# Rounding part of the eight-bit codes inside the attention's self half instead of ahead of it

## The chip, the cores and the metric

One Trainium2 chip, one core. The metric is device time in microseconds (us) of one execution, median of the runs shown. PE is TensorE, DVE is VectorE, ACT is ScalarE, POOL is GpSimd, SP issues most of the transfers.

## What is computed

The kernel is a two-layer decoder on x [16, 128, 256] and a context [16, 128, 256]. The change lies in one sublayer, the quantised attention of the second layer. Cut to what matters:

```
def _div_clamp_fp8(x, scale):
    y = jnp.clip(x / scale, -448, 448).astype(bfloat16)
    return y.astype(float8_e4m3fn)
q, k, v = (linear(_div_clamp_fp8(ln(x), s_j), w_j) for j in ("q", "k", "v"))   # self
qx      =  linear(_div_clamp_fp8(ln(x), s_qx), w_qx)                            # cross queries
kx, vx  =  split(ctx @ w_kv_x)
core = gqa(ln(q), ln(k), v);  xout = gqa(ln(qx), ln(kx), vx)
out  = _div_clamp_fp8(concat(core, xout), smooth) @ wproj
```

So the same normalised rows are divided by four different scale vectors and rounded to eight-bit floats, which gives four arrays of codes: query, key, value and cross query.

## The kernel before, in words

`quant_layer` runs two parts one after the other, with a barrier of all engines between them.

`round_codes` makes all codes. `XT` holds the normalised rows turned, as 2 blocks of 128 channels by 2048 tokens. There are 4 x 2 = 8 arrays (code kind by block, index n), each of 2048 columns in four tiles of 512. ACT scales an array into bf16 (L1531). DVE clamps it, takes its power of two by a mask, and makes the magic number of it (L1549, L1554, L1562, in halves of 1024). PE adds y + m - m in PSUM with three products per tile (L1521 to L1523), which does the rounding. ACT copies two of the four tiles to `xq` (L1541), DVE the other two (L1579).

`attention` runs 128 units: 8 head groups w, and for each the 16 batches b; units 0 to 63 are the self half, 64 to 127 the cross half. `in_steps` writes the order by hand: in step s each engine runs its list of stages, each for unit s minus its lag. PE: queries(s), keys_values(s), turn_p(s-3), turn_q(s-1), turn_k(s-1), output(s-5), values(s-3), scores(s-1). Every engine runs in its own order and waits on semaphores only. The PSUM banks of queries and keys have one buffer: PE's queries of unit n+1 wait until `apply_q` of unit n (L2003) has read the bank, and keys_values until `apply_kv` (L2010) has. The chain inside a step is: PE queries and keys, DVE statistics (L1992, L1997), POOL variance and power (L1947, L1952), DVE `apply_q` and `apply_kv`. Before `apply_q`, DVE runs magic (L2039), reciprocals, rounding (L2043) and residual (L2047) of older units. ACT turns queries and keys out of PSUM (L1866, L1874) for PE's scores (L1779). POOL then normalises the probabilities (L1956) and subtracts in rounded (L1963).

Of the kernel before, what the change touches and what calls it, by code (L numbers as in the profile page):

```python
# [18 lines left out]
P = 128  # L19
# [31 lines left out]
WHOLE = 1.5 * 2.0 ** 23  # L51

# [74 lines left out]
def build(nc, io, stop=99):  # L127
    ctx = ExitStack()
    with ctx:
# [13 lines left out]
        def sbuf(c, name, shape, dt):  # L143
            return c.enter_context(nc.sbuf_tensor(name, shape, dt))
# [22 lines left out]
        with ExitStack() as rows_ctx:  # L167
            XT = sbuf(rows_ctx, "XT", [P, CB, TOK], F32)
            args = dict(nc=nc, io=io, sem=sem, sbuf=sbuf, X=X, XT=XT, small=small, ident=ident, ps=ps,
                        col=col, cols=cols)  # L170
            with ExitStack() as routed_ctx:
# [1292 lines left out]
def quant_layer(row_stats, quant, rows_stored, w2_stored, nc, io, sem, sbuf, **args):  # L1464

    args = dict(nc=nc, io=io, sem=sem, sbuf=sbuf, **args)
    XT, cols, col = args["XT"], args["cols"], args["col"]
    ctx = ExitStack()
    with ctx:
        xq = sbuf(ctx, "xq", [P, 4, CB, TOK], F32R)  # L1470
        with ExitStack() as inner:
            round_codes(inner, xq, quant, **args)

        attention(xq, row_stats, quant, rows_stored, w2_stored, **args)


def round_codes(ctx, xq, quant, nc, io, sem, sbuf, X, XT, small, ident, ps, col, cols):

    N = 4 * CB
# [5 lines left out]
    p2 = sbuf(ctx, "p20", [P, 2, TOK], BF16)  # L1485
    m = sbuf(ctx, "m0", [P, 2, TOK], BF16)
# [8 lines left out]
    def bank(n, q):  # L1495
        return ps[(n * TILES + q) % 8][:, :]

    with nc.Block() as block:
# [10 lines left out]
        def _(pe):  # L1509
# [100 lines left out]
def attention(xq, row_stats, quant, rows_stored, w2_stored, nc, io, sem, sbuf, X, XT, small, ident, ps, col, cols):  # L1610
# [15 lines left out]
    with ctx:  # L1626
# [10 lines left out]
        spare = XT[:, :, :].rearrange("p k n -> p (k n)")  # L1637
# [17 lines left out]
        d_c = [sem(f"u_dc{k}") for k in range(4)]  # L1655
        names = ("cst", "chi", "clo", "q", "kv", "stat", "var", "rstd", "qn", "kvn", "tq", "tk", "qt", "kt", "sc", "neg",
# [23 lines left out]
        with nc.Block() as block:  # L1680
            @block.sync
            def _(sp):
# [20 lines left out]
                def load_context(u):  # L1703
# [132 lines left out]
            def _(act):  # L1836
                def context_high(u):
# [69 lines left out]
                in_steps([(turned_q, 2), (turned_k, 2), (prepare, 0), (context_high, 0), (scaled, 4), (row_normed, 8), (exps, 2),  # L1907
# [4 lines left out]
            def _(pool):  # L1912
# [3 lines left out]
                pool.wait_ge(s_cst, 3)  # L1916

# [61 lines left out]
                in_steps([(rounded, 5), (row_deviation, 7), (deviation, 0), (prepare, 0), (context_low, 0), (normalise, 2)])  # L1979

            @block.vector
            def _(dve):
                dve.wait_ge(s_cst, 3)

# [68 lines left out]
                def row_moments(u):  # L2053
                    if u.last:
# [4 lines left out]
                          (magic, 4), (reciprocals, 2), (rounding, 4), (residual, 5), (apply_q, 0)])  # L2059
# [655 lines left out]
```

## Time and profile before

| | us |
|---|---|
| median of 3 runs | 1412.66 |
| lowest, highest | 1412.54, 1413.17 |
| span of the profiled execution | 1411.1 |
| `round_codes`, first to last instruction | 341.94 to 370.84 |
| first PE instruction of attention | 371.58 |
| one step in the middle of the self half, PE's queries to PE's queries (568.44 to 574.10) | 5.66 |

The profiled execution has no time of its own in the records beside its span; the median of the runs is 1.6 us above that span, which is what lies around the first and the last instruction. In timelines a row is: start in us, duration in us, engine, line, operation, output<-inputs, shape, count; in brackets the idle time before it and what ended it.

### The profile page before, as it was taken

The page shows a single profiled execution, that of the slowest core. Times are in us where ns is not written, and L with a number is a line of the kernel's source. Part 1 is how long each engine was busy: PE and PEld are TensorE (multiplying, and loading weights), DVE is VectorE, ACT ScalarE, POOL GpSimd, SP SyncE. Part 2 cuts the span into 40 slices and gives each one's busy share as a digit, 9 for nine tenths or more (in the row PEclk, how much of TensorE's full clock was granted, in tenths as well). Part 3 has the DMA queues.
Part 4 walks back from the last instruction along what each step waited for, and adds up shares of the span by engine and source line. Part 5 has one row for each costly group of instructions (what it writes and reads, how often), then busy time and mean ns, then how long its engine had stood idle before and what let it go on. Part 6 is the DMA issues. An engine that isn't in the chain of part 4 may idle for free. (4 is left out here: it accounts for less than half of the span.)

```text
span 1411.1 us, 28423 instructions
## 1 busy us (share of the span) xinstructions
PE 1322.5 (94%) x8507; PEld 1098.8 (78%) x8507; DVE 1073.4 (76%) x2567; ACT 944.4 (67%) x3181; POOL 909.4 (64%) x1101
## 2 busy tenths in 40 slices
PE   9999988896799999999999999999999978999992
PEld 4445666663499999999999989998998855889882
DVE  5899768897788888888998888888888847444443
ACT  3997457776488787888887777777777746332331
POOL 4996237774178687786887767766867844455542
PEclk9999999998999999999999999999999999999996
DMA  9421110000101002002011020020100149577665
GB/s 341 158 117 63 36 46 2 1 2 1 60 1 62 29 2 98 1 31 69 24 61 53 1 91 2 1 91 2 46 1 24 68 144 340 138 168 162 164 162 134
DMA packets 55160, 105.85 MB, mean 75 GB/s; under 512 B 5052, under 2 KB 33668, under 8 KB 52708
## 3 DMA queue, kind: packets, MB, share of 16 engines
q1 hardware_dynamic: 46100, 84.90, 17.5%
q0 software_dynamic: 7488, 10.23, 4.5%
q10 hardware_dynamic: 1424, 8.91, 1.5%
q8 instruction: 73, 1.20, 0.4%
q14 instruction: 75, 0.61, 0.1%
HBM read 75.58 MB, written 28.44 MB: 74 GB/s over the span
## 5 line engine op out<-in xcount | busy, mean ns | idle before, releaser
L1882 ACT ACTIVATE pr_<-ps,neg_ 128x128 f32<-128x128 f32 x512 | 181.3, 366 | 64.5 <-DVE neg_ L2017 64.5
L1899 ACT ACTIVATE y<-ps,invsm 128x128 bf16<-128x128 f32 x512 | 146.4, 369 | 61.5 <-PE ps L1797 61.3
L1952 POOL TENSOR_TENSOR rstd<-var,half 128x6 f32<-128x6 f32 x128 | 172.3, 1346 | 10.1 <-POOL var L1947 0.2
L1963 POOL TENSOR_TENSOR z<-t,m 128x512 fp32r<-128x512 f32 x128 | 148.8, 1163 | 3.3 <-DVE t L2043 3.3
L1947 POOL TENSOR_TENSOR var<-stat,deps 128x6 f32<-128x6 f32 x128 | 26.0, 203 | 184.2 <-DVE stat L1997 184.2
L1779 PEld LDWEIGHTS ps<-qkt 128*128 128x128 f32 x1024 | 134.0, 191 | 10.3 <-ACT qkt L1866 2.7
L1808 PE MATMUL ps<-phi,z 128*128 128x256 f32 x512 | 138.2, 303 | 1.2 <-POOL z L1963 1.2
L1779 PE MATMUL ps<-qkt 128*128 128x128 f32 x1024 | 135.3, 275 | 2.3 <-ACT qkt L1874 2.1
L1797 PE MATMUL ps<-XT 128*128 128x256 f32 x512 | 131.8, 380 | 2.9 <-ACT XT L1890 2.8
L1956 POOL TENSOR_TENSOR pr_<-pr_,rec_ 128x512 f32<-128x512 f32 x128 | 133.5, 1043 | 1.4 <-DVE rec_ L2024 1.4
L1808 PE MATMUL ps<-plo,z 128*128 128x256 f32 x512 | 127.3, 279 | 0.0
L1992 DVE BATCH_NORM_STATS2 stat<-ps 128x6 f32<-128x256 f32 x256 | 97.7, 423 | 29.1 <-PE ps L1732 28.2
L2498 POOL DMA_INDIRECT sums<-f_ys,f_ids x39 | 61.8, 1585 | 88.7 <-PE ps L2354 43.4
L1731 PE MATMUL ps<-whi,xq 128*128 128x512 f32 x256 | 111.4, 435 | 4.7 <-DVE XT L2003 3.2
L1866 ACT ACTIVATE qkt<-ps,aff 128x512 f32<-128x512 f32 x128 | 99.0, 773 | 11.3 <-PE ps L1762 11.3
L1882 ACT ACTIVATION_READ_ACCUMULATOR pr_<-ps,neg_ 128x1 f32 x512 | 103.8, 203 | 0.0
L1732 PE MATMUL ps<-wlo,xq 128*128 128x512 f32 x256 | 100.8, 394 | 0.0
L1890 ACT ACTIVATE XT<-ps 128x512 f32<-128x512 f32 x128 | 76.5, 598 | 36.0 <-PE ps L1788 32.6
L2047 DVE SCALAR_TENSOR_TENSOR X<-ps,pscale,X 128x256 f32<-128x256 f32 x128 | 61.9, 484 | 47.8 <-PE ps L1808 47.6
L1808 PEld LDWEIGHTS ps<-phi,z 128*128 128x128 f32 x512 | 96.4, 188 | 2.2 <-POOL z L1963 1.7
L1808 PEld LDWEIGHTS ps<-plo,z 128*128 128x128 f32 x512 | 97.1, 190 | 0.1
L1797 PEld LDWEIGHTS ps<-XT 128*128 128x128 f32 x512 | 87.3, 189 | 11.2 <-ACT XT L1890 4.4
(357 smaller groups left out, 4023.8 us busy)
## 6 DMA issues: line engine op xcount, KB each, us to landing
f_w_low<-w_low SPq DMA_DIRECT2D x39, 512.0 KB, 3.6
centred<-raw_weights ACTq DMA_DIRECT2D x8, 1024.0 KB, 3.9
w_low<-w_dram SPq DMA_DIRECT2D x8, 1024.0 KB, 10.6
aw_st<-centred SPq DMA_DIRECT2D x7, 1024.0 KB, 6.1
raw_weights<-wself_dram SPq DMA_DIRECT2D x4, 1024.0 KB, 13.8
raw_weights<-wcross_dram SPq DMA_DIRECT2D x4, 1024.0 KB, 15.1
w_rest<-w_dram SPq DMA_DIRECT2D x8, 512.0 KB, 3.9
w_high<-w_top SPq DMA_DIRECT2D x8, 512.0 KB, 2.7
```

Of the source, the lines that this page charges most:

```text
L1731: pe.matmul(bQ[:, :], x[:, k, :], whi[:, u.slot, 0, k, :], start=(k == 0), stop=False)
L1732: mm = pe.matmul(bQ[:, :], x[:, k, :], wlo[:, u.slot, 0, k, :], start=False, stop=(k == CB - 1))
L1779: mm = pe.matmul(bS[:, h * S:(h + 1) * S], qkt[:, u.par, h, :], qkt[:, u.par, HEADS + h // 2, :], start=True, stop=True)
L1797: mm = pe.matmul(bO[:, two], kvn[:, u.place, 2 + w, :], pt[:, u.par, two], start=True, stop=True)
L1808: mm = pe.matmul(bW[:, 0:C], z[:, u.par, h * S:(h + 1) * S], part[:, u.slot, h // 2, h % 2, :], start=(h == 0 and part is phi), stop=(h == ...
L1866: act.activation(qkt[:, u.par, 0:HEADS, :], bTQ[:, :].rearrange("p (h s) -> p h s", h=HEADS), ACT.Identity, bias=a[:, 1:2], scale=a[:, 0:1 ...
L1882: ins = act.activation(pr[:, u.par, h, :], bS[:, h * S:(h + 1) * S], ACT.Exp, bias=neg[:, u.par, h:h + 1], accum_out=tot[:, u.par, h:h + 1])
L1899: ins = act.activation(y[:, u.par, h * S:(h + 1) * S], bO[:, h * S:(h + 1) * S], ACT.Copy, scale=invsm[:, head:head + 1])
L1952: pool.tensor_tensor(rstd[:, u.par, 0:6], v, half[:, :], ALU.pow).then_inc(s_rstd, 1)
L1956: pool.tensor_tensor(pr[:, u.par, :, :], pr[:, u.par, :, :], rec[:, u.par, :].unsqueeze(2).to_broadcast([P, HEADS, S]), ALU.mult).then_inc ...
L1963: pool.tensor_tensor(z[:, u.par, :], t[:, u.par, :], m[:, u.par, :], ALU.subtract).then_inc(s_z, 1)
L1992: dve.bn_stats(stat[:, u.par, 6 * h:6 * h + 6], two)
```

## The change

`round_codes` is cut to the query, key and value codes of batches 0 to 11: 6 arrays of 1536 columns in three tiles, of which ACT copies two and DVE one. The halves of DVE are 512 and 1024 columns. What is left is 14 pieces of 512 columns: the query, key and value codes of batches 12 to 15 (6 pieces), and all cross query codes (8 pieces). Each piece is now done inside the attention's self half without PE: ACT scales it (`late_scaled`), DVE clamps, masks, makes the magic number and adds (four instructions), and POOL subtracts (`late_rounded`) one step later. Piece i lies at step 2i for i below 6, then at steps 12, 16, 20 and so on to 40. The scratch of a piece is the raw context buffer, which is not in use yet; the first load of the context waits for the last piece. PE waits for the 6 self pieces at unit 12 and for all 14 at unit 64. The cross codes go to a tensor `xcross` that takes the place of `XT`. The attention's small buffers that lay in `XT` get a tensor of their own, `spare`.

```diff
--- before.py
+++ after.py
+EARLY = 3 * W512
+LATE_SELF, LATE = 3 * CB, 3 * CB + CB * NTG
...
@@ quant_layer @@
-        xq = sbuf(ctx, "xq", [P, 4, CB, TOK], F32R)
+        xq = sbuf(ctx, "xq", [P, 3, CB, TOK], F32R)
         with ExitStack() as inner:
             round_codes(inner, xq, quant, **args)
 
-        attention(xq, row_stats, quant, rows_stored, w2_stored, **args)
+        columns_ctx.close()
+        xcross = sbuf(rows_ctx, "xcross", [P, CB, TOK], F32R, side="right")
+        attention(xq, xcross, row_stats, quant, rows_stored, w2_stored, **args)
@@ round_codes @@
-    N = 4 * CB
-    TILES = TOK // W512
-    BY_ACT = TILES // 2
-    HALF = TOK // 2
-    halves = [slice(h * HALF, (h + 1) * HALF) for h in range(2)]
-    y = sbuf(ctx, "y0", [P, 3, TOK], BF16)
...
+    N = 3 * CB
+    TILES = EARLY // W512
+    BY_ACT = TILES // 2 + 1
+    halves = [slice(0, W512), slice(W512, EARLY)]
+    y = sbuf(ctx, "y0", [P, 3, EARLY], BF16)
...
-                    pe.wait_ge(s_magic, 2 * n + q // 2 + 1)
+                    pe.wait_ge(s_magic, 2 * n + min(q, 1) + 1)
@@ attention @@
-        spare = XT[:, :, :].rearrange("p k n -> p (k n)")
+        spare = sbuf(ctx, "spare", [P, 8 * UW], F32)
...
+        late_raw = raw[:, :, :, :].rearrange("p i k s -> p (i k s)")
+        late_y, late_m = (late_raw[:, i * C:(i + 1) * C].bitcast(BF16) for i in range(2))
+        late_t = late_raw[:, W512:2 * W512]
+
+        def late(u, after):
+
+            i, off = divmod(u.n - after, 2) if u.n - after < 2 * LATE_SELF else divmod(u.n - after + 2 * LATE_SELF, 4)
+            return i if off == 0 and 0 <= i < LATE else None
+
+        def late_place(i):
+
+            if i < LATE_SELF:
+                return i // CB, i % CB, slice(EARLY, TOK)
+            q, k = divmod(i - LATE_SELF, CB)
+            return CROSS, k, slice(q * W512, (q + 1) * W512)
...
+                    if u.n == EARLY // S:
+                        pe.wait_ge(s_late_z, LATE_SELF)
+                    if u.n == SELF:
+                        pe.wait_ge(s_late_z, LATE)
...
+                def late_scaled(u):
+                    i = late(u, 0)
+                    if i is None:
+                        return
+                    if i:
+                        act.wait_ge(s_late_z, i)
+                    j, k, at = late_place(i)
+                    act.activation(late_y, XT[:, k, at], ACT.Copy, scale=quant.inv[:, j, k:k + 1]
+                                   ).then_inc(s_late_y, 1)
...
-                in_steps([(turned_q, 2), (turned_k, 2), (prepare, 0), (context_high, 0), (scaled, 4), (row_normed, 8), (exps, 2),
+                in_steps([(late_scaled, 0), (turned_q, 2), (turned_k, 2), (prepare, 0), (context_high, 0), (scaled, 4), (row_normed, 8), (exps, 2),
...
+                def late_rounded(u):
+                    i = late(u, 1)
+                    if i is None:
+                        return
+                    j, k, at = late_place(i)
+                    pool.wait_ge(s_late_t, i + 1)
+                    pool.tensor_tensor(xcross[:, k, at] if j == CROSS else xq[:, j, k, at], late_t, late_m, ALU.subtract
+                                       ).then_inc(s_late_z, 1)
...
-                in_steps([(rounded, 5), (row_deviation, 7), (deviation, 0), (prepare, 0), (context_low, 0), (normalise, 2)])
+                in_steps([(rounded, 5), (row_deviation, 7), (late_rounded, 0), (deviation, 0), (prepare, 0), (context_low, 0), (normalise, 2)])
...
+                    dve.wait_ge(s_late_y, i + 1)
+                    dve.tensor_scalar(late_y, late_y, FP8_MAX, -FP8_MAX, ALU.min, ALU.max).then_inc(s_late_clamp, 1)
...
+                    dve.wait_ge(s_late_clamp, i + 1)
+                    dve.tensor_scalar(late_m.bitcast(U16), late_y.bitcast(U16), 0x7F80, None, ALU.bitwise_and
+                                      ).then_inc(s_late_p2, 1)
...
+                    dve.wait_ge(s_late_p2, i + 1)
+                    dve.tensor_scalar(late_m, late_m, FP8_MIN_NORMAL, ROUND, ALU.max, ALU.mult).then_inc(s_late_m, 1)
...
+                    dve.wait_ge(s_late_m, i + 1)
+                    dve.tensor_tensor(late_t, late_y, late_m, ALU.add).then_inc(s_late_t, 1)
...
-                          (magic, 4), (reciprocals, 2), (rounding, 4), (residual, 5), (apply_q, 0)])
+                          (late_clamp, 0), (magic, 4), (late_power, 0), (reciprocals, 2), (late_magic, 0), (rounding, 4),
+                          (residual, 5), (late_rounding, 0), (apply_q, 0)])
```

Vector engine, one step of the attention (step 6 of the change). In these rows `bQ`, `bKV` and the other banks read `ps`, and the change's `raw_context` is the late scratch (`late_y`, `late_m`, `late_t`). Before:

```order
L1997 BN_STATS stat<-ps 128x6
L2034 TENSOR_SCALAR m<-y 128x512
L2039 TENSOR_SCALAR m<-m 128x512
L2024 RECIPROCAL rec_<-tot 128x4
L2043 TENSOR_TENSOR t<-y,m 128x512
L2047 SCALAR_TENSOR_TENSOR X<-ps,pscale,X 128x256
L2003 TENSOR_TENSOR XT<-ps,rstd 128x512
L2010 TENSOR_TENSOR XT<-ps,rstd 128x512
```

In the change, the same stretch of a step that carries a piece of late rounding:

```order
L2072 BN_STATS stat<-ps 128x6
L2109 TENSOR_SCALAR m<-y 128x512
L2036 TENSOR_SCALAR raw_context<-raw_context 128x512
L2114 TENSOR_SCALAR m<-m 128x512
L2043 TENSOR_SCALAR raw_context<-raw_context 128x512
L2099 RECIPROCAL rec_<-tot 128x4
L2051 TENSOR_SCALAR raw_context<-raw_context 128x512
L2118 TENSOR_TENSOR t<-y,m 128x512
L2122 SCALAR_TENSOR_TENSOR X<-ps,pscale,X 128x256
L2058 TENSOR_TENSOR raw_context<-raw_context 128x512
L2078 TENSOR_TENSOR spare<-ps,rstd 128x512
L2085 TENSOR_TENSOR spare<-ps,rstd 128x512
```

Four instructions on `raw_context` (`late_clamp`, `late_power`, `late_magic`, `late_rounding`) now stand between the key statistics and the two multiplications that free the query bank and the key-value bank (`apply_q`, `apply_kv`: `XT<-ps,rstd` before, `spare<-ps,rstd` now).

Scalar engine, start of a step (the row after `turned_p`). Before:

```order
L1890 ACTIVATE XT<-ps 128x512
L1866 ACTIVATE qkt<-ps,aff 128x512
L1874 ACTIVATE qkt<-ps,aff 128x256
L1899 ACTIVATE y<-ps,invsm 128x128 x4
L1882 ACTIVATE pr_,tot<-ps,neg_ 128x128 x4
```

In the change:

```order
L1927 ACTIVATE spare<-ps 128x512
L1871 ACTIVATE raw_context<-XT,inv 128x512
L1903 ACTIVATE qkt<-ps,aff 128x512
L1911 ACTIVATE qkt<-ps,aff 128x256
L1430 ACTIVATE phi<-aw_rows 128x512
```

`late_scaled` now stands ahead of `turned_q` and `turned_k`, the two rows that write `qkt` for PE's scores.

## Rows read from the trace of the kernel before

**Rows 1.** The page: span, and the busy time of PE

```profile
span 1411.1 us, 28423 instructions
PE 1322.5 (94%) x8507; PEld 1098.8 (78%) x8507; DVE 1073.4 (76%) x2567; ACT 944.4 (67%) x3181; POOL 909.4 (64%) x1101
```

**Rows 2.** The view of windows, 100 us of the self half: busy time by engine

```profile
500.00:600.00 100.00, 100.00 (x745) 95.19 (x745) 87.64 (x215) 81.76 (x277) 75.36 (x81) 1.00 0.10 36
```

**Rows 3.** The view of waits, self half, 400 to 700 us

```profile
DVE X L2047 <- PE ps L1808: 18.6, 51, 0.4
```

**Rows 4.** The timeline of `round_codes`: start us, us, engine, line, tile

```profile
341.94 5.98 ACT L1531 ACTIVATE y<-XT,inv 128x1024 bf16<-128x1024 f32 x4 [2.64 <-PEq L141]
346.05 0.76 DVE L1549 TENSOR_SCALAR y<-y 128x1024 bf16<-128x1024 bf16 x2 [0.32 <-ACT y L1531]
354.49 1.28 DVE L1579 CAST xq<-ps 128x512 fp32r<-128x512 f32 x2
355.69 0.75 DVE L1549 TENSOR_SCALAR y<-y 128x1024 bf16<-128x1024 bf16 x2
369.50 1.34 DVE L1579 CAST xq<-ps 128x512 fp32r<-128x512 f32 x2 [0.68 <-PE ps L1523]
```

**Rows 5.** Instruction groups of `round_codes` by shape: count, busy us, mean ns

```profile
L1531 ACT ACTIVATE y<-XT,inv 128x1024 bf16<-128x1024 f32 x2 | 2.2, 1142 | 2.6 <-PEq L141 2.6
L1531 ACT ACTIVATE y<-XT,inv 128x2048 bf16<-128x2048 f32 x7 | 13.9, 2005 | 0.0
L1521 PE MATMUL ps<-y,plus 128*128 128x512 bf16 x32 | 12.7, 397 | 2.4 <-DVE m L1562 2.0 <-ACT xq L1541 0.4
```

**Rows 6.** The timeline of one step in the middle of the self half

```profile
565.58 0.29 DVE L2039 TENSOR_SCALAR m<-m 128x512 bf16<-128x512 bf16 x1
565.71 1.35 POOL L1952 TENSOR_TENSOR rstd<-var,half 128x6 f32<-128x6 f32 x1
565.90 0.69 DVE L2043 TENSOR_TENSOR t<-y,m 128x512 f32<-128x512 bf16 x1
566.51 0.57 ACT L1874 ACTIVATE qkt<-ps,aff 128x256 f32<-128x256 f32 x1
566.97 0.48 DVE L2047 SCALAR_TENSOR_TENSOR X<-ps,pscale,X 128x256 f32<-128x256 f32 x1 [0.37 <-PE ps L1808]
567.02 1.04 POOL L1956 TENSOR_TENSOR pr_<-pr_,rec_ 128x512 f32<-128x512 f32 x1
567.37 0.68 DVE L2003 TENSOR_TENSOR XT<-ps,rstd 128x512 f32<-128x512 f32 x1
567.63 1.05 PE L1779 MATMUL ps<-qkt 128*128 128x128 f32 x8
568.44 0.47 PE L1731 MATMUL ps<-whi,xq 128*128 128x512 f32 x1
574.10 0.47 PE L1731 MATMUL ps<-whi,xq 128*128 128x512 f32 x1
```

**Rows 7.** The timeline of attention's first step: `apply_q`, then PE's next queries

```profile
376.00 0.69 DVE L2003 TENSOR_TENSOR XT<-ps,rstd 128x512 f32<-128x512 f32 x1 [1.82 <-POOL rstd L1952]
376.75 0.50 PE L1731 MATMUL ps<-whi,xq 128*128 128x512 f32 x1 [3.03 <-DVE XT L2003]
```

**Rows 8.** The timeline at three places where DVE and POOL overlap

```profile
25.28 2.34 POOL L563 TENSOR_TENSOR XT<-hid,xin 128x1024 f32<-128x1024 f32 x1 [2.66 <-DVE hid L630]
26.71 1.06 DVE L779 TENSOR_TENSOR pr<-wf 128x128 f32<-128x128 f32 x1
...
677.49 1.17 POOL L1963 TENSOR_TENSOR z<-t,m 128x512 fp32r<-128x512 f32 x1
677.86 0.94 DVE L2028 TENSOR_SCALAR y<-y 128x512 bf16<-128x512 bf16 x1
...
1128.40 0.72 POOL L1972 TENSOR_TENSOR row_scale<-row_spread,half 128x1 f32<-128x1 f32 x1
1128.48 0.28 DVE L2028 TENSOR_SCALAR y<-y 128x512 bf16<-128x512 bf16 x1
```

More of the change, by code:

```diff
@@ L166, in build @@
         io["centred"] = nc.dram_tensor("centred", (2 * PAIRS, P, PIECES, UW), F32, kind="Internal").ap()
-        with ExitStack() as rows_ctx:
-            XT = sbuf(rows_ctx, "XT", [P, CB, TOK], F32)
+        with ExitStack() as rows_ctx, ExitStack() as columns_ctx:
+            XT = sbuf(columns_ctx, "XT", [P, CB, TOK], F32, side="right")
             args = dict(nc=nc, io=io, sem=sem, sbuf=sbuf, X=X, XT=XT, small=small, ident=ident, ps=ps,
@@ L1529, in scaled @@
                     act.wait_ge(s_z, (n - 2) * TILES)
-                for h in (halves if n == 0 else [slice(0, TOK)]):
+                for h in (halves if n == 0 else [slice(0, EARLY)]):
                     act.activation(y[:, n % 3, h], XT[:, n % CB, h], ACT.Copy,
@@ L1655, in attention @@
         d_c = [sem(f"u_dc{k}") for k in range(4)]
+        s_late_y, s_late_clamp, s_late_p2, s_late_m, s_late_t, s_late_z = (
+            sem("u_late_" + n) for n in ("y", "clamp", "p2", "m", "t", "z"))
         names = ("cst", "chi", "clo", "q", "kv", "stat", "var", "rstd", "qn", "kvn", "tq", "tk", "qt", "kt", "sc", "neg",
@@ L1708, in load_context @@
                         sp.wait_ge(s_clo, b - 3)
+                    else:
+                        sp.wait_ge(s_late_z, LATE)
                     sp.dma_start(raw[:, b % 4, :, :], io["ctxT"].rearrange("(k p) n -> p k n", p=P)[
@@ L1983, in _, with late_clamp, late_power, late_magic @@
                 dve.wait_ge(s_cst, 3)
+                def late_clamp(u):
+                    i = late(u, 0)
+                    if i is None:
+                        return
+                    dve.wait_ge(s_late_y, i + 1)
+                    dve.tensor_scalar(late_y, late_y, FP8_MAX, -FP8_MAX, ALU.min, ALU.max).then_inc(s_late_clamp, 1)
+                def late_power(u):
+                    i = late(u, 0)
+                    if i is None:
+                        return
+                    dve.wait_ge(s_late_clamp, i + 1)
+                    dve.tensor_scalar(late_m.bitcast(U16), late_y.bitcast(U16), 0x7F80, None, ALU.bitwise_and
+                                      ).then_inc(s_late_p2, 1)
+                def late_magic(u):
+                    i = late(u, 0)
+                    if i is None:
+                        return
+                    dve.wait_ge(s_late_p2, i + 1)
+                    dve.tensor_scalar(late_m, late_m, FP8_MIN_NORMAL, ROUND, ALU.max, ALU.mult).then_inc(s_late_m, 1)
+                def late_rounding(u):
+                    i = late(u, 0)
+                    if i is None:
+                        return
+                    dve.wait_ge(s_late_m, i + 1)
+                    dve.tensor_tensor(late_t, late_y, late_m, ALU.add).then_inc(s_late_t, 1)
                 def query_statistics(u):
```

19 lines of the change are left out of this document (9 added, 10 removed).

## The prediction

> **What bounds the kernel now.** I read the page first: PE is busy 94% of a span of 1411.1 us [rows 1]. The view of windows then says where that share comes from: in the self half PE is busy for all 100 us of a window, DVE for 87.64, ACT for 81.76, POOL for 75.36 [rows 2]. The view of waits for that half has no wait of PE at all; DVE, the next fullest, waits for PE once a step, 51 times for 18.6 us, 0.37 us each [rows 3]. So PE streams without a pause, its step is 574.10 - 568.44 = 5.66 us [rows 6], and whatever makes PE wait there is lost for good. The two places of the change are thus priced in different ways: `round_codes` by the length of its chain, the self half by how far the new instructions push PE.
>
> **What is removed.** `round_codes` runs from 341.94 to 369.50 + 1.34 = 370.84, 28.9 us [rows 4]. DVE sets its pace: three array starts lie between 346.05 and 355.69, 3.21 us each, made of three pairs of 1024-column instructions up to the copies and 1.2 us of copies (354.49 to 355.69) [rows 4]. The pairs take (3.21 - 1.20)/3 = 0.67, so a 1024-column instruction costs 0.335 from start to start. A 512-column one costs 0.19 (0.28 alone [rows 8], less the 0.09 by which neighbours overlap). A new array has 0.335 + 0.19 = 0.53 three times, and one copy of 0.60: 2.18 us. ACT has 2.43 (1536 columns by the line through 1.142 for 1024 and 2.005 for 2048 [rows 5] are 1.57, less 0.1; two copies near 0.48 each), but runs two arrays ahead, as now. PE has nine products of 512 columns, and at 0.215 us each (its three per tile keep pace with eight banks now; 0.397 is the modelled length of one [rows 5], of which half overlaps) 1.94. So the new pace is DVE's, some 2.2 us. Starts: array 1 waits for ACT, which scales 512, 1024 and 1536 columns where it scaled 1024, 1024 and 2048, so it starts 0.8 us sooner than 346.05. Then PE's first tiles, at the low clock, hold back the copies of array 0 and array 2 starts near 348.5; three periods on, array 5 starts at 355.0, its last tile leaves PE near 358.5 and the last copy ends near 359.3. The stage ends 370.84 - 359.3 = **11.5 us** sooner. Bounds: if each array only lost the quarter of its columns and kept all else, 28.9 x (1 - 6/8) = 7.2 us; if all went with the tiles, 28.9 x (1 - 18/32) = 12.6. I stay at 11.5, since the walk through the stage is near the upper one.
>
> **What is added: 14 pieces in the self half.** Pieces 0 and 1, at steps 0 and 2, lie where DVE waits for POOL's power anyway (1.82 us in step 0 [rows 7]); four instructions of 0.28, 0.28, 0.28 and 0.69 us are 1.5 us. Free. The other 12 meet a PE that never waits.
>
> ACT: `late_scaled` takes 0.64 to 0.71 us (the line through rows 5 gives 0.71 for 512 columns), 0.6 from start to start, ahead of `turned_q` and `turned_k`. `turned_k` ends at 566.51 + 0.57 = 567.08 and PE's scores start at 567.63 [rows 6]; DVE to PE takes 0.06 when PE waits (376.69 to 376.75 [rows 7]). So 0.55 less 0.06 to 0.11 is margin, 0.6 is asked for: PE loses **0.15 us** (0 to 0.25).
>
> DVE: late_clamp, late_power and late_magic come between power and rounding. The first fills a gap between dependent instructions, the others cost 0.19 each: rounding starts at 566.40 for 565.90. It ends at 567.09, residual starts at 567.00 for 566.97, since the 0.37 of waiting for PE takes up the rest [rows 3, 6]. `late_rounding` is next, at 567.40, and `apply_q` behind it. Without more, it would start at 568.00 for 567.37, end at 568.68, and PE would start queries at 568.74 for 568.44: 0.3 us lost. POOL's `normalise` lies there, however: it starts at 567.02 and runs 1.04 us [rows 6], some 0.1 later here. Does it hold up a DVE addition of two SBUF inputs? The timeline has the case: L779 of 128 columns, started in the middle of POOL's L563, took 1.06 us and ended at 27.77, 0.15 after POOL's end at 27.62 [rows 8]. A mask or clamp in bf16 does the same: 677.86 to 678.80, POOL's end being 678.66 [rows 8]. I take this as the case: `late_rounding` passes its data only from POOL's end at 568.18, so it ends near 568.73, `apply_q` runs 568.64 to 569.32, PE starts at 569.38. PE loses **0.93 us** (0.3 if the two do not meet). POOL's `rounded` waits for it in turn, by 0.4 us; its next work, the variance, is 1.9 us off, and `late_rounded` (as long as L1963, 1.17 us) still ends ahead of it. Then the queue behind: `apply_kv`, `maxima` and the statistics are late by 0.9 against a PE that is late by the same, so one step clears it. No wait of PE at units 12 and 64 and none of SP's context loads is late: each piece ends one step after its start, well ahead.
>
> The 12 pieces cost 12 x (0.93 + 0.15) = **13.0 us**. Where POOL also splits weights in the step of a piece (steps 10, 12, 28), the split stands where normalise stood, and adds a little; it goes into the range.
>
> **The sum**, against the span: 1411.1 - 11.5 + 13.0 = 1412.6; with the 1.6 us around it, 1412.66 + 1.5 = **1414.2 us**. That is within 0.2% (2.8 us), about what a measurement of this kernel can tell from no change.
>
> The Trainium skill (SBUF — State Buffer, "SBUF: two separate sides") says that DVE and GpSimd share a port pair under an exclusive lock, taken by a DVE instruction in a 2-port mode or with two SBUF inputs, and held for the whole instruction; the loser blocks. For `late_rounding` rule and rows 8 agree; by the rule alone also late_power and late_magic would wait for POOL's power instruction, which is the second rival.
>
> **Rivals.**
>
> A, faster: the two engines do not meet at `late_rounding` (POOL's normalise starts after it, or lets it through). Then a piece costs 0.3 + 0.15 = 0.45, twelve 5.4 us, and the time is 1412.66 - 11.5 + 5.4 = 1406.6. For it: only one row shows a blocked two-input instruction of this kind. Against it: normalise has 0.25 us of lead. It decides when the cost of a piece falls under (11.5 - 2.8)/12 = 0.73 us.
>
> B, slower: POOL's power instruction (rstd, 565.71 to 567.06 [rows 6]) holds up the two bf16 instructions that now fall in it. Then late_power ends at 567.2, rounding at 568.2, `late_rounding` at 569.2, `apply_q` at 569.85, and PE starts 1.45 late; with ACT's 0.15, 1.6 a piece, 19.2 in all, and the time is 1412.66 - 11.5 + 19.2 = 1420.4. It decides from 14.3/12 = 1.19 us a piece. Against it: at 1128.40 POOL ran a power instruction of 0.72 us, the clamp started 0.08 later and took its usual 0.28 [rows 8], and DVE's L2043, of two SBUF inputs, takes 0.69 inside rstd [rows 6]. Such an instruction seems to take the port only briefly.
>
> C, slower by less: the prices are mine, but what follows costs more (POOL's splits at steps 10 to 13, a blocked clamp in the next step, two pieces in a row not recovered): 0.3 us more a piece, 1412.66 - 11.5 + 16.6 = 1417.8.
>
> D, the saving in `round_codes` is smaller, as PE's first tiles run at the low clock and the stage may fall to the bound of 7.2: 1414.2 + 4.3 = 1418.5. Little speaks for it.
>
> **How the numbers follow.** Forecast 0.37; A 0.25; B 0.08; C 0.24; D 0.06. Predicted: 1414.2. From A's side (1406.6 less 1 for the saving's upper bound) to B's: the range 1405.8 to 1419.0 leaves out B and something beyond A. The forecast's own range is 1411 to 1417. Faster by over 0.2%: 0.26 (A, a little of the forecast). Within: 0.37. Slower: 0.37.
>
> **What would show it.** In the changed profile: `round_codes` ends near 359.3, its DVE period is near 2.2; steps of 5.66 us without a piece and near 6.7 with one; a wait of PE (or its weight loads) for DVE's `apply_q` some 12 times, near 0.9 us, and for `qkt` near 0.15; `late_rounding` lasting 1.3 us for 0.69, ending half a microsecond after POOL's normalise; late_power and late_magic at 0.28 to 0.35 (at 1.3, B is right). `late_rounding` at 0.69 throughout is A. The cross half keeps its steps. The prediction is wrong if the stage's end is off by more than 1 us, or the pieces cost less than 0.7 or more than 1.3 us of PE each.

## The result: slower by 0.4%, where no change was forecast

The changed kernel takes 1417.61 us, median of 12 runs (1415.68 to 1423.68), beside 1413.59 for the kernel before (12 runs, 1412.45 to 1414.97). The ratio is 1.0039, 95% interval 1.0027 to 1.0052. The forecast was 1414.2; the time lies in the range, 3.4 us above it, on the side of slower.

The page of the changed kernel (span; busy time by engine), beside [rows 1]:

```profile
span 1415.5 us, 28363 instructions
PE 1318.9 (93%) x8448; PEld 1094.0 (77%) x8465; DVE 1086.0 (77%) x2601; ACT 943.6 (67%) x3189; POOL 932.1 (66%) x1115
```

The view of windows, 500 to 600 us, beside [rows 2] (busy time of PE, weight loads, DVE, ACT, POOL; granted clock, DMA share, GB/s). PE, busy for the whole window before, now stands still for 3 us of it; the clock is as it was:

```profile
500.00:600.00 100.00, 97.01 (x703) 89.86 (x702) 90.08 (x217) 79.71 (x261) 79.32 (x81) 1.00 0.09 33
```

The view of waits, 400 to 600 us (engine, line, what it waited for: us, times, longest), beside [rows 3]. There are ten waits for `apply_q` (L2078), which stood in no such view before, and ten short ones ahead of the scores (L1806):

```profile
PEld ps L1758 <- DVE spare L2078: 9.6, 10, 1.2
PE ps L1758 <- DVE spare L2078: 7.7, 10, 1.0
DVE X L2122 <- PE ps L1835: 6.8, 19, 0.4
PEld ps L1806 <- issue: 3.7, 10, 0.4
```

The timeline of the changed kernel at two places: `round_codes` (342.54 to 360.12), beside [rows 4], and one piece of late rounding, from the step before it (475 us on), beside [rows 6]. Start, duration, engine, line, what it does, and in brackets the idle time ahead:

```profile
342.54 4.70 ACT L1534 ACTIVATE y<-XT,inv 128x512 bf16<-128x512 f32 x4 [2.63 <-PEq L143]
...
350.84 0.68 DVE L1582 CAST xq<-ps 128x512 fp32r<-128x512 f32 x1
353.05 0.69 DVE L1582 CAST xq<-ps 128x512 fp32r<-128x512 f32 x1
355.26 0.68 DVE L1582 CAST xq<-ps 128x512 fp32r<-128x512 f32 x1
...
358.13 1.25 ACT L1544 ACTIVATE xq<-ps 128x512 fp32r<-128x512 f32 x2 [0.96 <-PE ps L1526]
359.43 0.69 DVE L1582 CAST xq<-ps 128x512 fp32r<-128x512 f32 x1 [1.27 <-PE ps L1526]
...
476.74 0.71 ACT L1871 ACTIVATE raw_context<-XT,inv 128x512 bf16<-128x512 f32 x1
478.01 0.57 ACT L1911 ACTIVATE qkt<-ps,aff 128x256 f32<-128x256 f32 x1
478.65 0.97 PEld L1806 LDWEIGHTS ps<-qkt 128*128 128x128 f32 x8 [0.37 <-issue]
478.68 1.13 PE L1806 MATMUL ps<-qkt 128*128 128x128 f32 x8
479.56 0.48 PE L1758 MATMUL ps<-whi,xq 128*128 128x512 f32 x1
482.50 1.45 POOL L1998 TENSOR_TENSOR rstd<-var,half 128x6 f32<-128x6 f32 x1
482.69 0.28 DVE L2043 TENSOR_SCALAR raw_context<-raw_context 128x512 uint16<-128x512 uint16 x1
483.00 0.30 DVE L2051 TENSOR_SCALAR raw_context<-raw_context 128x512 bf16<-128x512 bf16 x1
483.21 0.69 DVE L2118 TENSOR_TENSOR t<-y,m 128x512 f32<-128x512 bf16 x1
483.81 0.48 DVE L2122 SCALAR_TENSOR_TENSOR X<-ps,pscale,X 128x256 f32<-128x256 f32 x1
483.92 1.04 POOL L2002 TENSOR_TENSOR pr_<-pr_,rec_ 128x512 f32<-128x512 f32 x1
484.21 1.29 DVE L2058 TENSOR_TENSOR raw_context<-raw_context 128x512 f32<-128x512 bf16 x1
484.92 1.60 POOL L2009 TENSOR_TENSOR z<-t,m 128x512 fp32r<-128x512 f32 x1
485.43 0.68 DVE L2078 TENSOR_TENSOR spare<-ps,rstd 128x512 f32<-128x512 f32 x1
486.16 0.50 PE L1758 MATMUL ps<-whi,xq 128*128 128x512 f32 x1 [0.69 <-DVE spare L2078]
491.87 0.48 PE L1758 MATMUL ps<-whi,xq 128*128 128x512 f32 x1
```

`round_codes` ends with DVE's last copy at 359.43 + 0.69 = 360.12 (forecast 359.3), at 2.21 us an array (forecast 2.2). It also began 0.60 later than before, at 342.54, so it is 17.58 us long, for 28.90 before and 17.36 in the forecast. In the attention `late_rounding` (L2058) begins 0.29 us into POOL's normalise (L2002), takes 1.29 for its 0.69, and ends at 485.50, 0.54 after POOL's end. `apply_q` follows, and PE's queries start at 486.16, so this step is 6.60 long and the next 5.71. The views of three lines (number: shortest, median, longest in ns) say how far this holds for the other pieces. Of the 14 additions (L2058) the first three take 0.69 us, eight take 1.29, and three (steps 10, 12 and 28) take 1.52. The bf16 instructions beside POOL's power are never held up:

```profile
L2058 DVE TENSOR_TENSOR raw_context<-raw_context x14: 685/1292/1525, 364.3 to 603.8; 128x512 f32<-128x512 bf16 x14
...
L2043 DVE TENSOR_SCALAR raw_context<-raw_context x14: 281/286/294, 363.7 to 602.3; 128x512 uint16<-128x512 uint16 x14
...
L2051 DVE TENSOR_SCALAR raw_context<-raw_context x14: 293/296/297, 364.0 to 602.6; 128x512 bf16<-128x512 bf16 x14
```

**Where the time went.** PE's first queries product of each unit (L1731 before, L1758 now) gives the length of every step, and so the account of one profiled execution of each kernel, in us. "Stage" is from the first scaling of `round_codes` to PE's first queries; "rest" is from unit 127's queries to the end, the expert layers above all; it is taken from a span given to 0.1 us, so its second decimal says nothing.

| kernel | stage starts | stage | steps 0-4 | 5-42 | 43-58 | 59-63 | 64-126 | rest | span |
|---|---|---|---|---|---|---|---|---|---|
| before | 341.94 | 29.64 | 27.06 | 215.08 | 90.59 | 29.74 | 387.02 | 290.03 | 1411.1 |
| changed | 342.54 | 18.31 | 26.88 | 229.45 | 90.88 | 29.72 | 387.66 | 290.06 | 1415.5 |
| e1, no pieces | 343.81 | 20.37 | 27.32 | 215.84 | 90.88 | 29.72 | 387.67 | 290.09 | 1405.7 |
| e2, ACT behind | 344.23 | 18.49 | 28.09 | 227.27 | 90.88 | 29.72 | 387.70 | 290.32 | 1416.7 |
| e3, add first | 343.45 | 18.37 | 26.87 | 222.62 | 90.88 | 29.69 | 387.67 | 290.25 | 1409.8 |
| e4, both | 342.59 | 17.99 | 26.26 | 220.62 | 90.88 | 29.71 | 387.71 | 296.54 | 1412.3 |
| e5, before, XT right | 343.40 | 29.65 | 27.10 | 215.33 | 90.70 | 29.74 | 388.04 | 296.54 | 1420.5 |
| e6, spread | 342.47 | 18.48 | 28.90 | 221.31 | 90.86 | 29.73 | 387.66 | 296.59 | 1416.0 |
| e7, spread two | 342.74 | 18.26 | 26.87 | 219.07 | 90.88 | 29.73 | 387.66 | 289.69 | 1404.9 |
| e8, before, 1 KB pad | 342.11 | 29.70 | 26.80 | 215.08 | 90.58 | 29.75 | 387.04 | 290.14 | 1411.2 |
| e9, last self early | 341.85 | 18.23 | 26.87 | 217.72 | 90.88 | 29.70 | 387.68 | 296.17 | 1409.1 |
| e10, spare right | 344.02 | 18.50 | 28.52 | 218.92 | 90.77 | 29.69 | 388.09 | 296.49 | 1415.0 |
| e11, 8 KB pad | 341.62 | 18.21 | 26.84 | 218.55 | 90.59 | 29.72 | 387.67 | 289.80 | 1403.0 |

The two spans differ by 4.4 us: +0.60 at the stage's start, -11.33 in the stage, -0.18 in steps 0 to 4, +14.37 in steps 5 to 42, +0.91 in the attention behind them (0.29 - 0.02 + 0.64), and nothing to speak of (0.03) in the rest. The stage's start lies anywhere from 341.62 to 344.23 in these profiles, whatever the edit, so 0.60 is no effect of the change that one profile can show.

### The profile page after: what moved, and what is told of

Its sections match the earlier page's. It is cut to its first block and busy times, and to the rows that moved or that the text cites. A ratio compares the mean times of both kernels' runs of the same rounds, so it can differ in the third digit from the quotient of the medians.

```text
span 1415.5 us, 28363 instructions
## 1 busy us (share of the span) xinstructions
PE 1318.9 (93%) x8448; PEld 1094.0 (77%) x8465; DVE 1086.0 (77%) x2601; ACT 943.6 (67%) x3189; POOL 932.1 (66%) x1115
## 5 line engine op out<-in xcount | busy, mean ns | idle before, releaser
L2009 POOL TENSOR_TENSOR z<-t,m 128x512 fp32r<-128x512 f32 x128 | 152.4, 1191 | 3.3 <-DVE t L2118 3.3
L1806 PEld LDWEIGHTS ps<-qkt 128*128 128x128 f32 x1024 | 133.1, 191 | 14.4 <-issue 4.9
L1806 PE MATMUL ps<-qkt 128*128 128x128 f32 x1024 | 136.1, 276 | 3.1 <-ACT qkt L1911 2.4
L2002 POOL TENSOR_TENSOR pr_<-pr_,rec_ 128x512 f32<-128x512 f32 x128 | 135.2, 1056 | 1.4 <-DVE rec_ L2099 1.4
L1824 PE MATMUL ps<-spare 128*128 128x256 f32 x512 | 131.8, 379 | 2.9 <-ACT spare L1927 2.8
L1927 ACT ACTIVATE spare<-ps 128x512 f32<-128x512 f32 x128 | 76.8, 600 | 36.1 <-PE ps L1815 33.0
L2092 DVE TENSOR_REDUCE neg_<-ps 128x4 f32<-128x512 f32 x128 | 88.2, 689 | 11.0 <-PE ps L1806 4.8
L1824 PEld LDWEIGHTS ps<-spare 128*128 128x128 f32 x512 | 87.6, 188 | 11.3 <-ACT spare L1927 4.4
L1146 POOL TENSOR_TENSOR d_pr<-d_pr,rec 128x512 f32<-128x512 f32 x64 | 68.2, 1072 | 40.8 <-DVE rec L1334 40.5
L1279 ACT ACTIVATE d_pr<-ps,neg 128x128 f32<-128x128 f32 x256 | 89.6, 402 | 7.8 <-DVE neg L1325 7.8
## 6 DMA issues: line engine op xcount, KB each, us to landing
raw_weights<-wcross_dram SPq DMA_DIRECT2D x4, 1024.0 KB, 14.5
```

The source lines that it names most:

```text
L1279: ins = act.activation(pr[:, u.par, h, t, :], bS[h][:, t * P:(t + 1) * P], ACT.Exp, bias=neg[:, u.par, h, t:t + 1], accum_out=tot[:, u.par ...
L1806: mm = pe.matmul(bS[:, h * S:(h + 1) * S], qkt[:, u.par, h, :], qkt[:, u.par, HEADS + h // 2, :], start=True, stop=True)
L1824: mm = pe.matmul(bO[:, two], kvn[:, u.place, 2 + w, :], pt[:, u.par, two], start=True, stop=True)
L2002: pool.tensor_tensor(pr[:, u.par, :, :], pr[:, u.par, :, :], rec[:, u.par, :].unsqueeze(2).to_broadcast([P, HEADS, S]), ALU.mult).then_inc ...
L2009: pool.tensor_tensor(z[:, u.par, :], t[:, u.par, :], m[:, u.par, :], ALU.subtract).then_inc(s_z, 1)
L2092: dve.tensor_reduce(neg[:, u.par, :], bS[:, :].rearrange("p (h s) -> p h s", h=HEADS), AX.X, ALU.max, negate=True).then_inc(s_neg, 1)
```

## The experiments

**e1: the change without its pieces.** The late codes are zeros (they are left out, memsets stand for them), the rest is as changed.

```diff
+            pool.memset(xq[:, :, :, EARLY:TOK].bitcast(F32), 0.0)
-                in_steps([(late_scaled, 0), (turned_q, 2), (turned_k, 2), ...
+                in_steps([(turned_q, 2), (turned_k, 2), ...
-                          (late_clamp, 0), (magic, 4), (late_power, 0), (reciprocals, 2), (late_magic, 0), (rounding, 4),
-                          (residual, 5), (late_rounding, 0), (apply_q, 0)])
+                          (magic, 4), (reciprocals, 2), (rounding, 4),
+                          (residual, 5), (apply_q, 0)])
```

> The changed kernel without the 14 pieces: late_scaled, the four late DVE instructions and late_rounded are left out, so the codes of batches 12 to 15 and all cross codes are zeros (written by memsets: of the self codes in round_codes, of the cross codes 8 times 512 columns on POOL in the idle time before the variance). It measures the shorter stage alone. My account from the two traces: the stage saves 10.7 us, the first steps another 1.1 us since the clock does not fall after the barrier, and the pieces cost some 15 to 16. So it should be 11 to 12 us faster than before (ratio near 0.992), with every step from 5 on at 5.66 us. Rival: a slowdown of 0.01 to 0.02 us in every step from step 25 on (5.68 for 5.66, 6.13 for 6.11 in the changed kernel's profile) comes from the new places of the buffers; then it is there in this run too, and 1 us of the gain is missing. If that is an effect of one execution, the steps are 5.66 to the end.

Measured: 1406.62 (1404.45 to 1412.76), ratio 0.9954, 0.9937 to 0.9972: 7.0 us faster than before. The expectation was 11 to 12. The table says what is missing of 11: the memset stands ahead of POOL's constants and holds up PE's first products, so the stage is 20.37 and not 18.31 (a fault of the experiment, 2.1 us). The rest is a finding: with no piece in it, every step from 5 to 58 is 5.68 us, not 5.66, and the cross half is 387.67, not 387.02. That is 0.76 + 0.29 + 0.65 = 1.7 us which the rest of the change costs, and the prediction had at nothing.

**e2, e3, e4: the order of the instructions.** e2 puts `late_scaled` behind both turns on ACT, e3 puts `late_rounding` ahead of `residual` on DVE, e4 does both.

```diff
-                in_steps([(late_scaled, 0), (turned_q, 2), (turned_k, 2), (prepare, 0), ...
+                in_steps([(turned_q, 2), (turned_k, 2), (late_scaled, 0), (prepare, 0), ...   # e2, e4
-                          (residual, 5), (late_rounding, 0), (apply_q, 0)])
+                          (late_rounding, 0), (residual, 5), (apply_q, 0)])                    # e3, e4
```

> The changed kernel with late_scaled moved on ACT from ahead of turned_q to behind turned_k, where ACT waits 0.75 us for PE. My theory: in the changed kernel the step before a piece's takes 5.90 for 5.66, because PE's scores wait for qkt; these steps go back to 5.66, 12 times 0.24, about 3 us faster than the changed kernel. Rival: the 0.24 us is PE waiting for something else (the DVE of the step before); then nothing changes.

> The changed kernel with late_rounding moved on DVE from behind residual to ahead of it, 0.4 us sooner; the same instructions, the same count. My theory is the port: at its new place it starts before POOL's normalise, takes 0.69 us and not 1.29, and POOL's normalise is the one that is held up. PE then waits 0.3 us a piece for apply_q where it waited 0.94: steps of 6.0 for 6.60, 12 times 0.6, about 7 us faster than the changed kernel. Rival: DVE simply has 1.3 us more work in a step and 0.37 of it is hidden, wherever the addition stands; then the step stays at 6.60 and the time within 1 us.

> Both moves together. If the two waits are separate, the gains add: about 10 us faster than the changed kernel, 1407, that is 6 us faster than before (ratio 0.996). If they cover each other, it is no better than the better of the two.

Measured: e2 1416.22 (1414.06 to 1422.48), ratio 1.0015, 1.0000 to 1.0030; e3 1410.80 (1409.15 to 1420.51), ratio 0.9985, 0.9964 to 1.0005; e4 1407.63 (1405.98 to 1419.87), ratio 0.9961, 0.9940 to 0.9982. e3 is 6.8 us below the changed kernel, as the meeting of DVE and POOL asked for; its rival, 1.3 us of DVE work wherever the addition stands, falls. The timeline of e3 for the same kind of step (start, duration):

```profile
477.48 0.48 PE L1758 MATMUL ps<-whi,xq 128*128 128x512 f32 x1
...
481.74 0.69 DVE L2058 TENSOR_TENSOR raw_context<-raw_context 128x512 f32<-128x512 bf16 x1
481.85 1.48 POOL L2002 TENSOR_TENSOR pr_<-pr_,rec_ 128x512 f32<-128x512 f32 x1
482.35 0.48 DVE L2122 SCALAR_TENSOR_TENSOR X<-ps,pscale,X 128x256 f32<-128x256 f32 x1
482.74 0.68 DVE L2078 TENSOR_TENSOR spare<-ps,rstd 128x512 f32<-128x512 f32 x1
...
483.48 0.50 PE L1758 MATMUL ps<-whi,xq 128*128 128x512 f32 x1
```

`late_rounding` now starts ahead of normalise, and it is POOL that is held up (1.48 for 1.04 us), which costs nothing. The step is 6.00 for 6.60. What remains of the piece is DVE's own work, 0.34. e2's median is only 1.4 us lower, but its steps are clear: the step before a piece falls from 5.90-5.94 to 5.66-5.70 (step 3 from 5.94 to 5.32), and steps 5 to 42 from 229.45 to 227.27. That is 2.2 us less and not 2.6, because steps 6 and 12 are 0.2 longer than in the changed kernel. Its first steps took 28.09 for 26.88, with a granted clock of 0.68 and 0.63 from 365 to 375 us. That does not go with the edit: e4 has it too, and took 26.26 there at 1.00. The two gains in steps 5 to 42 add up: 2.2 and 6.8 apart, 8.8 in e4.

**e5 and e8: the kernel before, its buffers moved.** e5 puts `XT` at the right end of SBUF as the change does, and nothing else. e8 leaves 1 KB a partition empty ahead of the attention's later buffers.

```diff
-            XT = sbuf(rows_ctx, "XT", [P, CB, TOK], F32)
+            XT = sbuf(rows_ctx, "XT", [P, CB, TOK], F32, side="right")    # e5
+        pad = sbuf(ctx, "pad_", [P, 256], F32)                            # e8
```

> The kernel before with one difference: XT is allocated from the right end of the memory, as in the changed kernel, nothing else. In all profiles of the changed kernel and its variants the plain steps of the attention take 5.68 us for 5.66 and the cross half 387.7 us for 387.0, 1.2 to 1.7 us in all. Theory: the place of the buffers that PE and the others read in the attention (before, the small buffers lay in XT) does it; then it is here too, steps of 5.68, and about 1.5 us slower than before. Rival: it comes from the rest of the change (other buffers at other places, the longer program); then the steps stay at 5.66 and the time is that of before within 1 us.

> The kernel before with an unused buffer of 1 KB per partition ahead of the attention's other buffers, so that all that are allocated after it lie 1 KB further on; XT and the codes stay. Nothing else changes. Theory: a step of 5.66 or 5.68 us hangs on where the buffers lie; if the small shift is enough, the steps or the cross half's 387.0 us move by 0.3 us or more in all. Rival: only the move of XT to the right end does it (387.0 to 388.0 us there); then this run has the times of before, step for step, within 0.2 us over each half. It also gives a second profile of the stages ahead of round_codes with XT at its old place: 341.9 us if the later starts (342.5 to 344.2) of the other profiles come from XT's place, later if they vary by themselves.

Measured: e5 1421.02 (1414.97 to 1422.17), ratio 1.0036, 1.0019 to 1.0053; e8 1413.86 (1412.68 to 1422.51), ratio 0.9999, 0.9985 to 1.0014. Moving one tensor costs: steps 5 to 42 +0.25, 43 to 58 +0.11, the cross half +1.02, 1.4 us in all. The other 6 us of e5's median are not in the attention: its rest takes 296.54 for 290.03. The view of windows of the three kernels, 1180 to 1210 us, where the expert layers begin (columns as above, PE first, the granted clock third from the end). The changed kernel:

```profile
1180.00:1210.00 30.00, 26.75 (x148) 20.62 (x148) 20.05 (x25) 17.46 (x22) 14.41 (x15) 1.00 0.68 258
```

e5:

```profile
1180.00:1210.00 30.00, 27.79 (x116) 21.59 (x116) 16.31 (x18) 13.32 (x17) 12.58 (x12) 0.77 0.62 233
```

e10, told of below:

```profile
1180.00:1210.00 30.00, 27.79 (x119) 21.13 (x119) 15.04 (x18) 9.69 (x18) 10.79 (x9) 0.85 0.45 158
```

In all five profiles with a long rest (e4, e5, e6, e9, e10) the granted clock is under 1.00 there, so that part of the work runs at the lower level of the clock; in the others it is 1.00. That the other runs of a kernel fall into the same two forms is read from their times alone, since only one run of each has a trace. On that reading a median is a mix of two times some 6 us apart: of e5's ten runs three are at 1414.97 to 1415.30 and seven at 1420.61 to 1422.17; of the changed kernel's twelve, eight are at 1415.68 to 1418.66 (median 1417.19) and four at 1420.89 to 1423.68. By the eight alone the change costs 3.6 us.

**e6, e7, e9: the pieces spread over more steps.** On top of e4, e6 lets `late_rounding` run one step after the magic number, so that no step has all four DVE instructions, and at unit 12 PE waits for each kind of codes on its own. On POOL it puts `late_rounded` behind the deviation in the same step. e7 puts it back and one step later. e9 takes the subtraction of piece 5, for which PE waits at unit 12, one step ahead. In all three the waits that guard the scratch move with the instructions: ACT waits for the addition of the piece before, DVE's mask for its subtraction. Those lines are left out here.

```diff
-                    i = late(u, 0)
+                    i = late(u, 1)                          # late_rounding: e6, e7, e9
-                in_steps([(rounded, 5), (row_deviation, 7), (late_rounded, 0), (deviation, 0), ...
+                in_steps([(rounded, 5), (row_deviation, 7), (deviation, 0), (late_rounded, 0), ...   # e6
-                    i = late(u, 1)
+                    i = late(u, 2)                          # late_rounded, in the old order: e7, e9
+                in_steps([..., (deviation, 0), (last_self, 0), ...                                   # e9
```

> The kernel with both moves, and the piece spread over two steps: late_clamp, late_power and late_magic stay in step n, late_rounding goes to step n+1 on DVE (ahead of residual), late_rounded to step n+1 on POOL behind the power instruction. Theory: what is left of a piece's cost in PE (0.33 us in its step) is DVE's work of 1.1 us against 0.37 us of waiting and 0.33 of margin in one step; 0.5 and 0.6 us in two steps both fit, so piece steps go to 5.70 and the time falls by 3 to 4 us more, to 1404. Rival: POOL, which now has the subtraction between power and normalise, is late with rounded and holds up DVE's clamp in the steps with weight splits (odd steps 3 to 13, 21 to 29, and so on); then those steps grow by 0.5 us and more, and it is no faster than with both moves.

> As the spread one, but late_rounded on POOL stands one step later again (step n+2, right behind rounded). Theory: DVE gains the same as there; but POOL's subtraction now follows the steps with weight splits (odd ones), so it runs into DVE's clamp of bf16, which waits for POOL's end (0.9 to 1.3 us for 0.28). Those piece steps cost 0.5 us or more of PE, so it is slower than the other spread kernel if that one's POOL place is fine, near 1406. Rival: the clamp has room, and both spread kernels agree within 1 us.

> The kernel with both moves, pieces over two steps and late_rounded two steps on, with one difference: the last self piece's subtraction is made one step sooner, behind POOL's power instruction of step 11. In the kernel without it step 12 takes 7.71 us, since PE waits for that subtraction. Theory: the wait of 2.0 us goes and the subtraction's place costs 0.5 (as it does at six places of the other spread kernel), so 1.5 us faster, near 1405.2. Rival: PE's wait at step 12 has another cause (the weight split of step 11 holds POOL up either way); then step 12 keeps 7 us or more.

Measured: e6 1410.17 (1408.59 to 1418.52), ratio 0.9987, 0.9965 to 1.0009; e7 1406.69 (1405.71 to 1407.01, 4 runs), ratio 0.9952, 0.9936 to 0.9969; e9 1411.16 (1405.44 to 1413.71), ratio 0.9964, 0.9949 to 0.9980. e6 was to be at 1404 and is not, as its rival said: a new wait takes the place of the old one. The view of waits of e6, 380 to 600 us:

```profile
PE ps L1817 <- POOL pr_ L2004: 2.7, 10, 0.5
```

POOL's queue now has `late_rounded`, a part of the weights' split and normalise in a row, and PE's turn of the probabilities is late. In the trace, all ten steps from 6 to 42 in which POOL runs both take 6.19 to 6.39, the two with `late_rounded` alone (18 and 34) 5.68 and 5.67, and those with a split alone 5.66 to 5.72. With POOL's part one step later (e7) the pieces cost nothing in most steps, though e7 was expected to be the slower of the two. Steps 6, 8, 10 and 28 keep 0.24 to 0.26; in the first three of them POOL's subtraction holds up a bf16 mask of DVE, which takes 0.84 or 0.85 us for 0.28. The timeline of e7 at step 12 and in two plain steps:

```profile
428.51 0.50 PE L1758 MATMUL ps<-whi,xq 128*128 128x512 f32 x1
431.92 0.39 PE L1781 MATMUL ps<-whi,xq 128*128 128x256 f32 x1 [1.76 <-POOL xq L1963]
436.22 0.48 PE L1758 MATMUL ps<-whi,xq 128*128 128x512 f32 x1
...
447.58 0.48 PE L1758 MATMUL ps<-whi,xq 128*128 128x512 f32 x1
453.26 0.48 PE L1758 MATMUL ps<-whi,xq 128*128 128x512 f32 x1
```

Step 12 is 7.71 us long, since PE waits for the last of the six self pieces. e9 brings it to 6.39, and steps 5 to 42 from 219.07 to 217.72. Eight of its twelve runs have the long rest, so its median says nothing of that; its four other runs are at 1405.44 to 1406.70, e7's at 1405.71 to 1407.01.

**e10 and e11: e7 with buffers moved again**, to see where the 0.02 us of a plain step comes from.

```diff
-        spare = sbuf(ctx, "spare", [P, 8 * UW], F32)
+        spare = sbuf(ctx, "spare", [P, 8 * UW], F32, side="right")    # e10
+        pad = sbuf(ctx, "pad_", [P, 2048], F32)                       # e11, ahead of raw_context
```

> As e7, but the buffer spare stands at the right end of SBUF, beside xcross, so the attention's buffers allocated after it (qkt, pr_, y, m, t, z) lie lower by its size. If the 0.02 us that a plain step lost in the change (5.66 before, 5.68 now, and the cross half 387.0 to 387.7) comes from where spare or the buffers behind it lie, the plain steps of this kernel differ from 5.68: at best 5.66 again, which gives back up to 1.5 us (1405.2 against 1406.7 for e7). If it comes from xq, xcross or anything allocated ahead of spare, the step stays at 5.68 and the cross half at 387.7.

> As e7, but 8 KB a partition left empty ahead of raw_context and all later buffers of the attention; xq, the weights and xcross keep their places. If plain steps depend on where the later buffers lie, they change from 5.68 us; if not, the step stays 5.68, the cross half 387.7, and the time is that of e7, 1406.7 within 1 us (or some 6 us more in executions where the expert layers begin at a lower granted clock).

Measured: e10 1409.98 (1404.69 to 1416.75), ratio 0.9959, 0.9933 to 0.9984; e11 1406.99 (1404.74 to 1409.86, 6 runs), ratio 0.9942, 0.9921 to 0.9964. The timeline of e11, two plain steps of 5.66 us:

```profile
446.33 0.48 PE L1759 MATMUL ps<-whi,xq 128*128 128x512 f32 x1
451.99 0.48 PE L1759 MATMUL ps<-whi,xq 128*128 128x512 f32 x1
```

8 KB of empty space bring steps 43 to 58 from 90.88 to 90.59, the value of before; in e10 they are 90.77, in steps of 5.67, 5.67 and 5.68. So the places of the attention's own buffers bear on the 0.02 us of a self step. They are not all of it: e9, whose buffers lie where e7's do, has plain steps of 5.66 from step 16 to 27, where e7 has 5.68. The cross half does not follow: 387.67 with the pad, 388.09 with `spare` at the right end, 387.02 before. Its 0.64 us stays unexplained. A kernel before whose only edit is a `spare` of its own was not run.

By their medians e7 and e11 are faster than both kernels: by 0.5% and 0.6% than before, by about 11 us than the change as it was made. They have only four and six runs, nearly all with the short rest; e9 and e10, close to the same kernel, have the long one in about half of theirs and are 0.4% faster than before.

## Why the forecast failed, step by step

- **The stage, -11.5: held.** 18.31 for 29.64, 11.33 less, its pace as forecast. Its end is 0.82 later than the forecast's 359.3; 0.60 of that is the later start, 0.22 the stage itself. Rival D falls.
- **DVE and POOL meet at `late_rounding`, 0.93 a piece: held.** The step is 6.60 for 5.66 (0.94), `late_rounding` takes 1.29, and e3 takes 0.60 of it away by changing one pair's order. Rival A falls, except at step 4: there the addition started 0.11 ahead of normalise, took 0.69, and the step grew by 0.29. Rival B falls too: late_power and late_magic take 0.29 and 0.30, with POOL's power instruction around them. The way to the 0.93 has one flaw: two instructions at 0.19 each are 0.38, and the start written down for rounding, 566.40 for 565.90, has 0.50; the trace has 0.53. The Trainium skill (SBUF — State Buffer, "SBUF: two separate sides") has a DVE instruction in a 2-port mode, or with two SBUF inputs, wait for the whole of a POOL instruction that started first; for POOL's product and subtractions of 512 columns this trace agrees, for its power instruction it doesn't.
- **ACT ahead of the turns, 0.15 a piece: mis-sized, and the largest miss.** The step before a piece takes 5.90 to 5.94, so it costs 0.24 to 0.28; step 3, where PE's step was 5.33, costs 0.61. The twelve come to 3.4 us, where the forecast had 1.8. That it is ACT's order is shown by e2, where it is gone. The margin was counted to the start of PE's products, 567.63. PE must load `qkt` as weights first, and before the change that started 0.22 sooner. The timeline of before:

```profile
567.41 1.08 PEld L1779 LDWEIGHTS ps<-qkt 128*128 128x128 f32 x8
```

  In the changed kernel loads and products start together (478.65 and 478.68 above), 0.07 behind `turned_k`. Within their steps the products start 0.17 later than before, and they take 1.13 for 1.05: 0.25 in all.
- **POOL's splits "into the range": left out of the sum.** Steps 10, 12 and 28 take 6.84, 6.88 and 6.84, another 0.24 to 0.28 each, 0.75 in all. The timeline of the changed kernel at step 10 shows why: the addition meets the weights' split of 1.27 us, not normalise of 1.04, and again ends 0.54 after it.

```profile
423.13 1.27 POOL L1434 TENSOR_TENSOR plo<-aw_rows,phi 128x512 fp32r<-128x512 f32 x1
423.42 1.52 DVE L2058 TENSOR_TENSOR raw_context<-raw_context 128x512 f32<-128x512 bf16 x1
```

  This is one part of rival C's mechanism. "One step clears it" is nearly right: the step after a piece keeps 0.02 to 0.05. C's blocked clamp is there too, in steps 5, 11, 13 and 29 (0.73 for 0.28), behind a late `late_rounded`; it costs little, for steps 13 and 29 with it take 5.71 and 5.68.
- **The failed step is thus the sum "12 x (0.93 + 0.15) = 13.0", by its ACT term above all:** steps 3 to 42 grew by 0.89 + 14.37 = 15.3. The twelve steps ahead of a piece have 3.4 of it (forecast 1.8), the twelve with a piece 11.5 (forecast 11.2: the splits add 0.75, step 4 falls short by 0.64, the rest is 0.04 at most in each), the others 0.4 (forecast 0). If the whole 0.76 that e1 shows without pieces is in it, 14.5 belong to the pieces. It may be less than 0.76, because a few plain steps (14, 18, 22) are 5.66 in the changed kernel.
- **Not in the forecast, a gain:** steps 0 to 2 take 15.35 for 16.42. Before, the second step took 6.22. The views of windows show why: before,

```profile
376.00:381.00 5.00, 4.25 (x18) 3.73 (x18) 2.48 (x5) 0.29 (x1) 0.56 (x2) 0.66 0.48 175
```

and changed,

```profile
365.00:370.00 5.00, 2.79 (x18) 2.39 (x19) 2.52 (x6) 1.96 (x3) 2.58 (x4) 1.00 0.56 206
370.00:375.00 5.00, 3.89 (x26) 3.34 (x26) 4.29 (x11) 2.72 (x11) 1.45 (x3) 1.00 0.00 0
```

  The granted clock is 0.66 in the one and 1.00 in the other. The change does not ensure it: e5 and e8, in the order of before, have the long second step (6.26, 6.02), but so have e1, e2, e6 and e10 (6.49, 6.94, 7.09, 7.08), while the changed kernel, e3, e4, e7, e9 and e11 take 5.07 to 5.44. What decides it was not found.
- **"The cross half keeps its steps": wrong.** It is 0.64 longer, and steps 43 to 58 are 0.29 longer with no piece in them. The forecast took the new places of the buffers for free. e1 shows both lengths with no piece in the kernel; e11 takes the 0.29 away by a pad, and e5 shows that moving one tensor can cost the cross half 1.02. What costs it 0.64 in the changed kernel is not shown.

Against the sum of +1.5 the profiles give 4.4: 0.2 from the stage, 2.3 from steps 3 to 42, -1.1 from the first three steps, 0.9 behind step 42, 0.6 from the stage's start. The time named for rival C, 1417.8, is close to the measured one, but C asked for 3.6 us more from the pieces, and they gave 1.5 to 2.3; the rest has other causes, so that C's time fits by luck.

## What to carry to other kernels

Work that is moved under an engine that never waits costs what its neighbours' order makes of it, not its length: fourteen pieces cost about 15 us in the order given and some 4 with a few of their instructions put elsewhere (e7), and the stage they came from gave 11. Look for each added instruction at what the other engines run at that moment, and put it where the one that can wait is the second to start. Count an engine's margin to the first thing that needs its result, here PE's weight loads and not its products. Compare the lengths of untouched steps before and after, too: they show costs of moved buffers that no wait shows.

## What the runs showed of the hardware

- When DVE's addition of two SBUF inputs and POOL's product of 512 columns overlap, the second to start is held up: DVE 1.29 for 0.69 us (changed), or POOL 1.48 for 1.04 (e3). The one that is held up ends 0.54 us after the other, behind an instruction of 1.04 us as behind one of 1.27 (changed, steps 6 and 10). POOL's power instruction holds up neither bf16 instructions (0.28 to 0.30) nor such an addition (0.69). It pays a little itself: it takes 1.45 us in the eleven piece steps from 6 to 40 of the changed kernel, with the late bf16 instructions beside it, and 1.33 to 1.35 in all others from 5 to 42.
- PE's step in a steady loop depends on where buffers lie in SBUF: 5.66, 5.67 or 5.68 us with the same instructions. 1 KB of padding changed nothing (e8), 8 KB turned 5.68 into 5.66 (e11). Two rhythms can stand in one execution, with the buffers where they are: in e9 plain steps are 5.66 up to step 27 and 5.68 from step 32. Why is open.
- The expert layers take 290 or 296.5 us, with the granted clock at 1.00 or below it at their start. How often the long form comes differs between kernels that differ only far ahead of it: in 7 of 10 runs of e5, 8 of 12 of e9, 5 of 10 of e10, 4 of 12 of the changed kernel, none of 4 of e7, at most one of 6 of e11, none of the 12 of before beside the changed kernel, 6 of the 85 of before beside the experiments. Runs without a trace are counted by their time. What decides it was not found.
